# The head of VectorE's step loop is placed at the first slot of an instruction block

## The reference, cut to what matters

```python
xn = layernorm(x)                                    # 12500 x 256
agg = segment_sum(xn[src] * edge_weight, dst)        # 212500 edges, sorted by dst
x = x + agg @ W.T + b
h = layernorm(x)
logits = gelu(h @ W1 + b1) @ Wg + bg                 # hidden 1024, 8 experts
e, p = argmax(softmax(logits)), max(softmax(logits))
out = x + p * (gelu(h @ W1 + b1) @ Wd[e] + bd[e])    # each node by its own expert
```

## Time and profile before

| | us |
|---|---|
| three runs | 4279.6, 4298.8, 4314.05 |
| median | 4298.8 |
| the profiled execution | 4314.99 |
| its span, first to last instruction | 4313.3 |
| busy PE | 2380.3 |
| busy POOL | 1733.8 |
| busy DVE | 1060.5 |

### The profile page before, as it was taken

The page is one execution under the profiler, slowest core; times in us unless marked ns, Lnnn a source line. Parts: engine busy times, 40 slices in busy tenths (PEclk is TensorE's granted clock), DMA queues, the critical chain, the costliest instruction groups (busy, mean ns, idle before and its releaser), DMA issues.

```text
span 4313.3 us, 46911 instructions
## 1 busy us (share of the span) xinstructions
PE 2380.3 (55%) x13404; PEld 1774.7 (41%) x13405; DVE 1060.5 (25%) x3850; ACT 698.0 (16%) x1711; POOL 1733.8 (40%) x1796
## 2 busy tenths in 40 slices
PE   0146555556555555664655674564664564655448
PEld 0135444434443334453444453343443443543348
DVE  7122222222222122222212222122222222212111
ACT  4002111111111111120110120110120120111123
POOL 2652444343444343434434425334335435342431
PEclk9867776767777777776776776777776776776679
DMA  8432333343234234234234324324324324324534
GB/s 322 127 110 94 91 122 105 92 129 118 70 118 136 69 120 127 76 105 137 72 115 132 88 88 145 95 84 136 97 87 137 101 84 141 104 78 150 177 126 161
DMA packets 199053, 503.10 MB, mean 117 GB/s; under 512 B 45096, under 2 KB 114347, under 8 KB 180688
## 3 DMA queue, kind: packets, MB, share of 16 engines
q0 software_dynamic: 88752, 244.13, 19.2%
q1 hardware_dynamic: 109472, 252.06, 17.7%
HBM read 442.89 MB, written 83.68 MB: 122 GB/s over the span
## 4 chain that ended last, share of the span: by engine, by line
PE 40%; another core or an unknown queue 26%; issue 24%; DVE 3%; ACT 2%; DVEq 2%; SPq 1%; DMA 1%; ACTq 0%; POOL 0%; POOLq 0%
PE psH L623 12%; PE psY L635 9%; PE psH L682 9%; PE psH L720 4%; PE psE L591 2%; PE psA L688 1%; PE psH L673 1%; SPq L380 1%; DVEq L296 1%; DVE stats L784 1%; PE psT L706 1%; ACT hidT L520 1%; DVE parts L1012 1%; PE psT L696 1%
## 5 line engine op out<-in xcount | busy, mean ns | idle before, releaser
L436 POOL DMA_INDIRECT big<-xn_table,src_i x1664 | 1608.5, 967 | 2271.6 <-PE psQ L582 1612.3
L591 PE MATMUL psE<-place,parts 128*128 128x80 f32 x832 | 207.5, 431 | 1051.8 <-DVE parts L1012 699.7
L591 PEld LDWEIGHTS psE<-place,parts 128*128 128x128 f32 x832 | 185.2, 328 | 1121.4 <-DVE parts L1012 752.8
L623 PE MATMUL psH<-work,w 128*128 128x128 f32 x3712 | 526.4, 310 | 103.5 <-ACT work L497 96.5
L623 PEld LDWEIGHTS psH<-work,w 128*128 128x128 f32 x3712 | 513.6, 224 | 112.1 <-issue 108.2
L682 PE MATMUL psH<-work,w 128*128 128x512 f32 (+1 forms) x800 | 405.7, 668 | 58.1 <-issue 25.0
L635 PE MATMUL psY<-big,hidT 128*128 128x256 f32 x1856 | 420.3, 379 | 3.5 <-ACT hidT L503 2.2
L582 PE MATMUL psQ<-big,sel_narrow 128*32 128x256 f32 x3328 | 295.3, 516 | 185.1 <-issue 144.6
L635 PEld LDWEIGHTS psY<-big,hidT 128*128 128x128 f32 x1856 | 343.6, 190 | 46.2 <-ACT hidT L503 2.7
L503 ACT ACTIVATE hidT<-psH,b 128x128 f32<-128x128 f32 x928 | 265.5, 370 | 544.7 <-PE psH L623 535.5
L1006 DVE TENSOR_TENSOR place<-iota,shift_f 128x160 f32<-128x160 f32 x104 | 34.0, 327 | 1178.3 <-issue 1178.3
(11 more groups left out here) (217 smaller groups left out, 1825.8 us busy)
## 6 DMA issues: line engine op xcount, KB each, us to landing
big<-in_Wd SPq DMA_DIRECT2D x116, 1024.0 KB
big<-xn_table,src_i POOLq DMA_INDIRECT x1664
expert_bins<-sorted_rows SPq DMA_DIRECT2D x375, 65.0 KB
xr<-expert_bins SPq DMA_DIRECT2D x116, 130.0 KB
big<-in_bd SPq DMA_DIRECT2D x116, 128.0 KB
big<-in_x SPq DMA_DIRECT2D x10, 1280.0 KB, 17.6
xn_table<-big SPq DMA_DIRECT2D x10, 1280.0 KB, 13.6
xg<-in_x SPq DMA_DIRECT2D x25, 512.0 KB
```

The source lines that it names most:

```text
L436: nc.gpsimd.indirect_dma_start(out=xring[:, h * STEP_TILES + j, :], out_offset=None, in_=xn_dram[:, :], in_offset=bass.IndirectOffsetOnAxi ...
L591: mm = nc.tensor.matmul(psE[:, at:at + SPAN], parts[:, o, k * P:(k + 1) * P], place[:, o, :], start=True, stop=True)
L623: mm = nc.tensor.matmul(psH[c // 4][:, (c % 4) * P:(c % 4 + 1) * P], w1[:, k, c * P:(c + 1) * P], xT2[i][:, k * P:(k + 1) * P], start=(k = ...
```

## The change

The loop over the steps on DVE is opened by the general form of the loop, for the one engine DVE, with a demand on where its head lies: slot 0 of an instruction block of that engine. Nothing in the loop's body differs.

```diff
-            with dve.Fori(0, STEPS) as k:
+            with nc.Fori(0, STEPS, engines=[DVE], head_slot={DVE: 0}) as k:
```

## The result

| | runs | median us | lowest to highest |
|---|---|---|---|
| before | 20 | 4285.52 | 4258.9 to 4314.05 |
| changed | 20 | 4320.64 | 4275.55 to 4351.41 |

The ratio is 1.007, with a 95% interval of 1.0045 to 1.0096: the change made the kernel 0.7% slower. The forecast was 4035, with a range of 3930 to 4260. The profiled execution has a span of 4334.5 us.

The account below looks back on a forecast made before the run. It took DVE's loop, fetched anew each turn, and completions held until POOL's burst landed as the limits. 24 × (6 + 5) + 11 = 275 us off 4314.99 gave 4040, 4035 as a median; range 3930 to 4260.

Parts of the forecast that it names:

- A: DVE's instruction memory holds fewer than four blocks, so the back edge still stalls; gain 105 us, about 4210; chance 0.20.
- C: The program doesn't get the placement, or the block's first slot lies elsewhere; 4300, five fetches a turn; chance 0.06.
- Step 1: From `part_b`'s end to `part_a`: line 659 comes about 5.2 us earlier; 6 us a group, bounds nothing to 9.7.
- Step 2: After `part_a`: DVE stands ready for line 582's release and starts line 1006 earlier; 5 us a group, bounds 2 to 7.
- Steps 3 and 4: Inside `part_a` and `part_b`: nothing; outside the groups, last gather steps without a burst: about two turns of 6, 11 us.
- D: Earlier DVE and PE work lengthens POOL's bursts by 0.5 us, 4367; slower beyond 2.5 us a burst; chance 0.04.
- B: Late completions are DVE's lateness, not the burst's hold; paces after `part_b` and `part_a` shrink, 672 us, about 3640; chance 0.04.

Follow-up runs that it names:

- e2: The kernel before with the gathers of all steps but the first three left out; 4096.49 us, 0.962 of the kernel before.
- e3: The changed kernel with the gathers of all steps but the first three left out; 3123.11 us, 0.7334 of the kernel before.
- e4: The changed kernel with POOL waiting in the middle of each burst until the first 8 gathers have landed; 3860.53 us, 0.906 of the kernel before.
- e16: The changed kernel with a pause after every fourth gather until issued gathers have landed, completions held; 3512.41 us, 0.8178 of the kernel before.
- e10: The changed kernel run once more without any edit, no completions held; 3098.13 us, 0.7491 of the kernel before.
- e8: The changed kernel with gathers after the third step bringing 16 of 256 columns, none held; 3075.72 us, 0.7439 of the kernel before.
- e17: The changed kernel with gathers of 16 columns in place of 256 after the third step, run again, none held; 3077.09 us, 0.7451 of before.
- e13: The changed kernel with its loop head at slot 12 in place of slot 0, completions held; 4326.35 us, 1.0074 of the kernel before.
- e15: The changed kernel with four small POOL memsets in the middle of each burst, completions held; 4325.4 us, 1.0037 of the kernel before.
- e12: The changed kernel with a pause after every fourth gather until issued gathers have landed, none held; 3337.24 us, 0.8075 of the kernel before.
- e9: The changed kernel with four small POOL memsets in the middle of each burst, none held; 3103.68 us, 0.7506 of the kernel before.

## Why the prediction was wrong

**What bounds the kernel.** The fetch stalls were rightly found and nearly rightly sized: 1178 us of issue fell to 262, 2.5 us a step where I had said under 2, with 60 packets where I had some 40. That completions of PE are held during bursts was right too, for the condition of those runs. That they come out only when the burst has landed was too simple: the copy at 1748.93 came before the train's end, and products early in a burst mostly weren't held (line 673, which ends 6.0 to 6.5 us into a burst of 16 in 11 groups, in one of them). What I did not see is that the two limits were nearly equal: e2 shows that the bursts added only some 4% to the time that the stalls alone give.

**The capacity.** The loads vanished as forecast, and rivals A and C are out: 60 packets in the whole execution, where A had about 630 and C 815. (A's sum was 120 us and I said 105, without a reason.) That the memory holds four blocks was my estimate, and no run shows it. What the runs show is 60 or 61 packets with the head at slots 0, 12 and 13 and 816 at slot 106, and slot 13 shows that my own count of blocks isn't exact. That some of a turn's packets are loaded ahead of their use can be seen in the trace before: one starts at 1627.35, in the straight code of `part_b`, and DVE's next two operations, at 1627.56 and 1627.65, start without a gap. Another falls between 1566.35 and 1566.55, beside line 1006 at 1566.52, and none from 1566.8 to 1571.7; the branch of line 1019, taken at 1570.52, costs 0.45 us. And the 8 KB that I read from the trace is the size of the packets of q14, not of all: q8 has 14 packets and 0.23 MB, some 16 KB each.

**Step 1, ahead of `part_a`: 24 × 6 us, got nothing.** ACT's idle time is 48.53 us against 48.34. Line 659 did move up, by 3.6 us where I had 5.2, but the transposes, done 16 us into the burst, were held until ACT's copy 23.1 us into it, where I had taken one group's 17.1 us as free. In the kernel before only 5 of the 24 groups were like that one (line 623 comes at most 1.1 us after the transposes, in the others 4.1 to 6.1 us). And SP, whose times I took as given, issued the tile's load 4.4 us later in the group. Over the whole execution PE's idle time fell by 70 us ahead of line 659 and by 19 ahead of line 623 and rose by 82 ahead of line 612: 7 us gained, where this step had 144. In these traces held completions have no fixed place in a burst; the row of one lucky group said nothing of the others.

**Step 2, after `part_a`: 24 × 5 us, and this is the step that failed.** In ten of 23 groups the 5 us were there, and more: 6.7 us less of waiting than the mean before. In the other thirteen the waiting grew by 9.5 us. I wrote that the lower bound was 2 us, "if ACT's gelus or the burst take the rest back". That bound had the wrong sign. Without the loads, DVE comes to its copy in time (it waits 754.8 us there, before 70.1), and then it depends on which completion is held. Where line 582's is held to the burst's end, the next burst starts late (3.30 us after the last gather in the group shown) and line 673 passes early in it, 6 us after its start. Where line 582's comes out sooner, POOL's two bursts join into 32 gathers with no gap between, and line 673 falls into the second half of this train, where ACT begins its two copies 15 to 21 and 21 to 24 us after the product's record ends. So the step treated line 673 as free to come earlier, "alongside the last burst", although the same hold stood in my own account of line 582. PE's idle time ahead of line 682 rose by 270 us. 237 saved and 270 lost is the result in its main part.

**Steps 3 and 4** were small. Step 3's "nothing" was wrong for the reason above.

**The rivals.** D had the right sign and the right place (work that comes earlier meets the bursts) but the wrong mechanism: gathers did not become longer (0.960 us in the mean, before 0.967); completions waited longer. Its point of decision, 2.5 us a burst, was of no use. B, that the hold is not the burst's, is refuted where completions are held (e3, e4, e16). Where they are not, the time falls even further than B had it: 3098 in e10 against 3640. The forecast was for the condition of the runs that it was read from; in the other it would have been as wrong, on the other side. I gave no chance to the hold being a condition of the machine; one profile could not show it.

**What stays open:** what sets the condition, and whether the hold hangs on the bytes moved or on gathers issued one right after another; e8 and e17 both fell where nothing was held. What in a pause lets completions out, the landing or its length, is open too. That the joined bursts are what holds line 673 in the changed kernel is read from the traces (12 of 12 groups with a joined train against 1 of 11 without; in e13 11 of 11 against none of 12) and fits e4 and e16, which part them. It was not tried by delaying the second burst alone, and a joined train isn't needed: in e15 four of the nine groups with a burst of 16 are held too, for 7.1 to 18.5 us.

**A version that beats both:** where completions are held, e16 (the change and three pauses a burst, two runs) is 18% faster than the kernel before and 19% faster than e13, the changed one with its head at slot 12; where none is held it is 19% faster than before (e12), and the changed kernel alone is faster still (e10, 25%).

## What to carry to other kernels

A stall, however large in the profile (here 1178.3 us of issue), can lie over another limit of the same height: before costing its removal, ask for each product that moves where in its neighbours' traffic it will land, and let the lower bound go below zero where it can land in a part that holds it. A small gap in a stream of transfers may be doing work: here one of some 2.5 us in each burst (e4) goes with 9.4% less time. And read a trace group by group: the mean of this one hides that ten groups gained what was forecast while thirteen lost more. When a kernel's time depends on such a condition, run the kernel before beside every experiment and read its time first; without that, e9 would have been taken for a cure.

## What the runs showed of the hardware that was not expected

- On one and the same program (e10 and the changed kernel of the prediction) completions of PE are taken by ACT, DVE and POOL either at once or late during bursts of indirect gathers (ACT's copies of line 673 up to 24.0 us after its record), and the time is 3098 or 4321 us. The gathers themselves look alike: 0.94 to 0.95 us each at 1.25 us distance in both.
- With waits of mostly 2.0 to 2.7 us in which issued gathers land, line 682 follows line 673 by at most 0.69 us (e4) and 3.1 us (e16), and DVE waits 355.2 and 96.5 us with "remote" as the releaser ahead of its copy; with 0.86 us between two gathers, filled with small work of POOL, it is up to 24.85 us and 743.5 us (e15).
- SP's 15 copies of sorted rows, where one row of the timeline has all of them, took 19.0 to 46.0 us in the changed kernel where completions are held (34.3 in the mean), and 15.8 to 16.6 us in e10.
- Where the loop is not loaded anew, issue ahead of line 1006 is 2.5 us a step (260.0 us in 104 steps, e10), where it was 11.3.
- The loop of 372 instructions is not loaded anew in each turn with its head at slots 0, 12 and 13 (60 or 61 packets), and it is with its head at slot 106 (816).
- TensorE's granted clock was 0.743 over the changed kernel's span, of which PE is busy 54%, and 0.836 over that of e10, of which it is busy 73%. Both are means over a span, and which follows from which was not tested.
